# The sum over source heads moved to one contraction on TensorE, with amplitudes and values turned through DRAM

## What is computed

```python
# per token: q, k, v of 8 heads x 16; each head normed; q and k "entangled" in 3 depths -> complex
for c in range(4):                                   # circuits
    pattern = einsum('bsid,bsjd->bsij', conj(qa), ka)
    scores  = abs(mod) ** 2 * SCALING
    amps    = sqrt(softmax(scores, axis=-1) + 1e-12) # (tokens, 8 target heads i, 8 source heads j)
    weighted = einsum('bsij,bsjd->bsid', w, vq)      # sum over source heads j
    co = weighted * coh                              # coh turns by the phase of the sum of vq over heads
    amp = clip(abs(co), 1e-6, 1.0)                   # magnitude clipped, sign kept
    final = final + sup_w[c] * amp * exp(1j * phase)
return real(final) @ W_out.T + b_out
```

## Time and profile before

| what | value |
|---|---|
| median of 3 runs | 2482.29 us (2481.22 to 2492.06) |
| span of the profiled execution | 2447.5 us |
| busy in it: PE / PEld / DVE / ACT / POOL | 1901.8 / 1470.5 / 1872.7 / 1264.7 / 1562.1 us |
| residual x0 loads (one at the end of each iteration) | 96.67, 153.42, 216.18, then 28 more until 1909.46 us |

### The profile page before, as it was taken

The page is one execution under the profiler, slowest core; times in us unless marked ns, Lnnn a source line. Parts: engine busy times, 40 slices in busy tenths (PEclk is TensorE's granted clock), DMA queues, the critical chain, the costliest instruction groups (busy, mean ns, idle before and its releaser), DMA issues.

```text
span 2447.5 us, 42464 instructions
## 1 busy us (share of the span) xinstructions
PE 1901.8 (78%) x14044; PEld 1470.5 (60%) x14044; DVE 1872.7 (77%) x3303; ACT 1264.7 (52%) x2982; POOL 1562.1 (64%) x1233
## 2 busy tenths in 40 slices
PE   1478888888888888888888888888888877968490
PEld 0366666666666666666666666666666654746370
DVE  8989999998999999999999989999998742311010
ACT  2246666555556655555565555555555544423130
POOL 4656666666666666666666666666666215788787
PEclk9889999898999998999998989999989876989795
DMA  3000000000000000000000000000000001233233
GB/s 96 5 5 10 9 9 9 9 9 9 9 9 9 9 9 9 9 9 9 9 9 9 9 9 9 9 9 9 9 9 6 8 10 39 46 41 41 47 36 33
DMA packets 66108, 39.50 MB, mean 16 GB/s; under 512 B 10886, under 2 KB 61967, under 8 KB 66064
## 3 DMA queue, kind: packets, MB, share of 16 engines
q0 software_dynamic: 22528, 16.79, 5.2%
q1 hardware_dynamic: 43490, 22.12, 3.2%
q10 hardware_dynamic: 46, 0.00, 0.0%
HBM read 22.11 MB, written 16.78 MB: 16 GB/s over the span
## 4 chain that ended last, share of the span: by engine, by line
POOL 30%; issue 25%; DVE 21%; PE 17%; ACT 6%; DVEq 1%; POOLq 0%; ACTq 0%; DMA 0%
POOL out_x L1246 7%; POOL arena L481 5%; POOL arena L677 4%; POOL arena L649 4%; DVE arena L831 4%; PE pb L1056 3%; POOL arena L478 2%; POOL arena L1236 2%; PE pa L752 2%; PE pa L779 2%; POOL arena L682 1%; DVE arena L578 1%; DVE arena L583 1%; POOL arena L483 1%; PE pa L1335 1%
## 5 line engine op out<-in xcount | busy, mean ns | idle before, releaser
L771 PE MATMUL pa<-ident,arena 128*128 128x128 f32 x4096 | 531.9, 287 | 56.9 <-DVE arena L649 52.9
L771 PEld LDWEIGHTS pa<-ident,arena 128*128 128x128 f32 x4096 | 504.1, 201 | 74.2 <-DVE arena L649 36.1
L1056 PE MATMUL pb<-ident,arena 128*128 128x128 f32 x1536 | 289.9, 302 | 128.1 <-ACT arena L951 119.0
L1056 PEld LDWEIGHTS pb<-ident,arena 128*128 128x128 f32 x1536 | 187.0, 152 | 246.0 <-issue 158.8
L951 ACT ACTIVATE arena<-pb 128x384 f32<-128x384 f32 x512 | 253.0, 494 | 157.6 <-PE pb L1056 153.8
L677 POOL TENSOR_TENSOR arena<-state,c_cross 128x448 f32<-128x448 f32 x128 | 202.5, 1602 | 203.8 <-DVE state L538 199.1
L669 POOL TENSOR_TENSOR arena<-arena,neg_half 128x32 f32<-128x32 f32 x64 | 264.9, 4158 | 83.8 <-DVE arena L515 83.8
L649 POOL TENSOR_TENSOR arena<-arena 128x1024 f32<-128x1024 f32 x64 | 149.9, 2343 | 197.0 <-PE pa L771 197.0
L944 ACT ACTIVATE arena<-pd,arena 128x256 f32<-128x256 f32 x512 | 245.6, 480 | 0.0
L649 DVE TENSOR_TENSOR arena<-arena 128x1024 f32<-128x1024 f32 x192 | 236.1, 1256 | 2.5 <-PE pa L771 2.2
L1246 POOL DMA_INDIRECT out_x<-arena x128 | 201.9, 1577 | 39.0 <-issue 37.1
(11 more groups left out here) (244 smaller groups left out, 4314.0 us busy)
## 6 DMA issues: line engine op xcount, KB each, us to landing
x_land<-in_L_attn_query SPq DMA_DIRECT2D x32, 128.0 KB, 2.1
arena<-in_L_attn_query SPq DMA_DIRECT2D x32, 128.0 KB, 2.1
out_x<-x SPq DMA_DIRECT2D x32, 128.0 KB, 1.8
xn_scratch<-xn_d SPq DMA_DIRECT2D x32, 128.0 KB, 1.8
w<-in_L_ffn_W SPq DMA_DIRECT2D x1, 2048.0 KB
arena<-xn_scratch,arena POOLq DMA_INDIRECT x128, 2.5
out_x<-arena POOLq DMA_INDIRECT x128, 3.3
arena<-in_L_attn_W_qkv SPq DMA_DIRECT2D x1, 192.0 KB, 2.7
```

The costliest lines, as they stand in the source:

```text
L771: mm = pe.matmul(pa[:, t, c * P:c * P + P], wprod[:, k % NWP, j * 128:j * 128 + 128], ident[:, :], start=(j == 0), stop=(j == NH - 1))
L1056: mm = pe.transpose(pb[:, j * P:j * P + P], p_raw[:, s % 3, j * P:j * P + P], ident[:, :])
```

## The change

1. **Values.** In stage C, DVE now computes the sign of the sum of the values and flips them first (lines 588 to 590 after), then SP writes `v_enc` to DRAM (`send_values`) and reads it back with 16 DMAs (`spread_values`) into `v_diag`: 16 groups of 16 tokens-and-tiles, partitions (x, t, j), values in block-diagonal columns. The zeros off the diagonal are written once, in the setup.
2. **Amplitudes.** ACT writes them as (tile, source, circuit x target); SP sends them to DRAM (`send_amps`) and reads them back with one DMA of 128 x 16 pieces of 32 words (`spread_amps`) into `amps_t`.
3. **The sum.** PE contracts the 128 partitions (8 tokens x 2 tiles x 8 sources) at once: 16 groups x 4 strips of 32 columns, 64 matmuls with 64 moving columns. The 8 products of DVE and POOL, their buffers and the 64 matmuls against the identity are gone.
4. **Layout after the sum.** The output projection reads every eighth word of `clipped` as its stationary operand, against weights reordered in the setup (`wout_q`). It waits for both clipped halves.
5. **Smaller parts.** `prod` is reused for both tiles, the third product has its own buffer; `norm_scale` waits until its factors have been applied; a wait is added ahead of stage B's first statistics; all four order strings are new.

```diff
-        mag = first("mag", [P, T, NC * P])
-        clipped = first("clipped", [P, T, NC * P])
-        prod = first("prod", [P, T, 3, 1024])
-        wprod = first("wprod", [P, NWP, 1024])
+        amps = first("amps", [P, T, NH, CI])
+        mag = first("mag", [P, 2, 512])
+        clipped = first("clipped", [P, 2, 512])
+        prod = first("prod", [P, 2, 1024])
+        prod_third = first("prod_third", [P, T, 1024])
+        v_diag = first("v_diag", [P, NGRP, XG * HD])
+        amps_t = first("amps_t", [P, NGRP, CI])
 
         x1 = first("x1", [P, T, E])
         state = sb("state", [P, 2, T, 2, E])
...
+            v.memset(v_diag[:, :, :], 0.0).then_inc(S("v_diag_zero"), 1)
...
             link(v.tensor_scalar(sup_w[:, :], tmp[:, 48:52], tmp[:, 53:54], None, ALU.mult))
+            by_d = wout_s.rearrange("p (i q d) -> p q i d", q=NQ, d=DQ)
+            for d in range(DQ):
+                v.tensor_tensor(wout_q[:, d, :].rearrange("p (q c i) -> p q c i", q=NQ, c=NC),
+                                by_d[:, :, :, d].unsqueeze(2).broadcast_to([P, NQ, NC, NH]),
+                                sup_w[:, :].unsqueeze(1).unsqueeze(3).broadcast_to([P, NQ, NC, NH]),
+                                ALU.mult).then_inc(S("w_out_scaled"), 1)
...
             if not (isinstance(b, int) and b == 0):
-                v.wait_ge(S("a_wprod"), 6 * b)
-                v.wait_ge(S("a_wpool"), 2 * b)
+                v.wait_ge(S("v_out"), 16 * b)
...
+
+            v4 = v_enc[:, :, :].rearrange("p t (i d) -> p t i d", d=HD)
+            v.wait_ge(S("a_venc"), b + 1)
+            yield from L(v.tensor_reduce(v_sum[:, :, :], v_enc[:, :, :].rearrange("p t (i d) -> p t d i", d=HD), AX, ALU.add))
+            yield from L(v.tensor_scalar(v_sign[:, :, :], v_sum[:, :, :].bitcast(U32), SIGN, None, ALU.bitwise_and))
+            v.tensor_tensor(v4.bitcast(U32), v4.bitcast(U32), v_sign[:, :, :].unsqueeze(2).broadcast_to([P, T, NH, HD]),
+                            ALU.bitwise_xor).then_inc(S("a_signed"), 1)
+            yield
 
...
             yield
-
-            v.wait_ge(S("a_amps"), b + 1)
-            for t in range(T):
-                for c in range(NC):
-                    k = t * NC + c
-                    if k and k not in ON_POOL:
-                        yield
-
-                    if k not in ON_POOL:
-                        if k >= NWP:
-                            v.wait_ge(S("a_wsum"), 8 * b + k - NWP + 1)
-                        weighted(v, t, c).then_inc(S("a_wprod"), 1)
-                    if k == 6:
-                        yield
-                        yield from vector_clip(v, b, 0)
-            yield
-            yield from vector_clip(v, b, 1)
-            yield
+            for h in range(2):
+                yield from vector_clip(v, b, h)
+                yield
             v.wait_ge(S("a_y"), b + 1)
 
             v.wait_ge(S("x0_bias"), b + 1)
...
-            for n, k in enumerate(ON_POOL):
-                g.wait_ge(S("a_amps"), b + 1)
-                g.wait_ge(S("a_wsum"), 8 * b + k - NWP + 1)
-                weighted(g, k // NC, k % NC).then_inc(S("a_wpool"), 1)
                 yield
             g.wait_ge(S("x0_in"), 16 * b + 16)
             g.tensor_tensor(x0[:, :, :], x0[:, :, :], bout_v.unsqueeze(1).broadcast_to([P, T, E]), ALU.add)\
...
-            for t in range(T):
-                act.wait_ge(S("a_wsum"), 8 * b + 4 * t + 4)
-                act.activation(mag[:, t, :], pa[:, t, :], ACT.Abs).then_inc(S("a_mag"), 1)
+            if not (isinstance(b, int) and b == 0):
+                act.wait_ge(S("amps_out"), 16 * b)
+            act.activation(amps[:, :, :, :].rearrange("p t j c -> p t c j"), probs[:, :, :].rearrange("p (t c) j -> p t c j", t=T),
+                           ACT.Sqrt, bias=tiny[:, 0:1]).then_inc(S("a_amps"), 1)
+            yield
+            for h in range(2):
+                act.wait_ge(S("a_wsum"), 2 * b + h + 1)
+                act.activation(mag[:, h, :], pa[:, h, :], ACT.Abs).then_inc(S("a_mag"), 1)
                 yield
 
...
         def tensor_c(pe, b):
-            for t in range(T):
-                for c in range(NC):
-                    k = t * NC + c
-                    if k:
-                        yield
-                    elif not (isinstance(b, int) and b == B - 1):
-                        pe.wait_ge(S("a_qkvb"), b + 2)
-                    if k == 0 and not (isinstance(b, int) and b == 0):
-                        pe.wait_ge(S("x2_ready"), b)
-                    if k in ON_POOL:
-                        pe.wait_ge(S("a_wpool"), 2 * b + k // NC + 1)
-                    else:
-                        pe.wait_ge(S("a_wprod"), 6 * b + k - k // NC + 1)
-                    for j in range(NH):
-                        mm = pe.matmul(pa[:, t, c * P:c * P + P], wprod[:, k % NWP, j * 128:j * 128 + 128], ident[:, :],
-                                       start=(j == 0), stop=(j == NH - 1))
-                    mm.then_inc(S("a_wsum"), 1)
-            for t in range(T):
-                yield
-                pe.wait_ge(S("a_clip"), 2 * b + t + 1)
-                o = pa[:, t, 0:128]
-                for c in range(NC):
-                    mm = pe.matmul(o, clipped[:, t, c * P:c * P + P], w_out_t[:, c, :], start=(c == 0), stop=(c == NC - 1))
+            if not (isinstance(b, int) and b == B - 1):
+                pe.wait_ge(S("a_qkvb"), b + 2)
+            if not (isinstance(b, int) and b == 0):
+                pe.wait_ge(S("x2_ready"), b)
+            pe.wait_ge(S("v_spread"), 16 * XG * b + 16 * XG)
+            pe.wait_ge(S("amps_spread"), 16 * b + 16)
+            for h in range(2):
+                for g in range(NGRP // 2):
+                    n = NGRP // 2 * h + g
+                    of_row = v_diag[:, n, :].rearrange("p (x d) -> p x d", d=HD)
+                    for q in range(NQ):
+                        mm = pe.matmul(pa[32 * q:32 * q + 32, h, g * 64:g * 64 + 64].rearrange("p (x d) -> p x d", d=DQ),
+                                       amps_t[:, n, :], of_row[:, :, DQ * q:DQ * q + DQ], start=True, stop=True)
+                mm.then_inc(S("a_wsum"), 1)
+                yield
+            pe.wait_ge(S("a_clip"), 2 * b + 2)
+            of_tile = clipped[:, :, :].rearrange("p h (n k) -> p (h n) k", k=T * DQ)
+            for t in range(T):
+                for d in range(DQ):
+                    mm = pe.matmul(pa[:, t, 0:128], of_tile[:, :, t * DQ + d], w_out_t[:, d, :], start=(d == 0), stop=(d == DQ - 1))
             mm.then_inc(S("a_y"), 1)
             yield
 
...
+        def send_values(sp, b):
+            if isinstance(b, int) and b == 0:
+                sp.wait_ge(S("v_diag_zero"), 1)
+            else:
+                sp.wait_ge(S("a_wsum"), 2 * b)
+            sp.wait_ge(S("a_signed"), b + 1)
+            sp.dma_start(v_rows_d, v_enc[:, :, :].rearrange("p t n -> p (t n)")).then_inc(S("v_out"), 16)
+
+        def spread_values(sp, b):
+            sp.wait_ge(S("v_out"), 16 * b + 16)
+            of_row = v_rows_d.rearrange("(g x) (t j d) -> (x t) j g d", x=XG // T, t=T, d=HD)
+            for x in range(XG):
+                sp.dma_start(v_diag[NH * x:NH * x + NH, :, HD * x:HD * x + HD], of_row[x]).then_inc(S("v_spread"), 16)
+
+        def send_amps(sp, b):
+            sp.wait_ge(S("a_amps"), b + 1)
+            sp.dma_start(amps_d, amps[:, :, :, :].rearrange("p t j c -> p (t j c)")).then_inc(S("amps_out"), 16)
+
+        def spread_amps(sp, b):
+            sp.wait_ge(S("amps_out"), 16 * b + 16)
+            sp.dma_start(amps_t[:, :, :], amps_d.rearrange("(g x) (t j c) -> (x t j) g c", x=XG // T, t=T, c=CI)).then_inc(S("amps_spread"), 16)
 
         def sync_d(sp, b):
...
+                load_x0(sp, b)
             with sp.Fori(3, B - 1) as b:
                 load_x(sp, b + 1)
+                send_values(sp, b - 1)
+                spread_values(sp, b - 1)
+                send_amps(sp, b - 1)
+                spread_amps(sp, b - 1)
```

110 lines of the change are left out of this document (57 added, 53 removed).

## The result

The changed kernel takes **2500.11 us** (median of 20 runs, 2480.07 to 2507.88) against 2483.7 us for the kernel before: a ratio of **1.006 (95% interval 1.0043 to 1.0076)**, slightly slower, where 2253 us was forecast. The profiled execution spans 2500.6 us.

The account below looks back on a forecast made before the run. The loop was taken as bound by DVE's row of work plus a short serial tail; period 60.47 to 53.0 us saves 209, filling 21, last 3, setup -4, together 229: 2253 us, forecast range 2200 to 2295 us.

Parts of the forecast that it names:

- PE can't be the bound by its sum: PE's work in the loop: falls from 50 to 38 us an iteration, so its total cannot set the period.
- rival 2: PE's clock in second attention: 1.2 GHz for longer, chain about 4 us longer, period 57, 2374 us; chance 0.12.
- Rival 1: Projection's strided operand, line 768: doubling line 779's 3.35 us, period 56.4, 2360 us; chance 0.13.
- The walk's path: One iteration followed from probabilities at 28.0 us through POOL's crosses and stage D's norm to a 53.0 us period.
- My own check: Last drain iteration but one, without A and C: lasts 53.00 us at clock 0.78, so period not below 51.
- Products, and DVE's row: Products removed from DVE: 7.3 us an iteration, plus 0.6 of POOL's hold-up, leaving DVE 47.3 of 55.2 us.
- The contraction: PE's 64 new matmuls: taken as 4.5 us an iteration, between 4.2 and 6.7, running from 40 to 44.5.
- Transfers: Trips through DRAM: amplitudes spread between 35.3 and 39.0 us, hidden by 1 to 5 us; values hidden by twenty.
- rival 4: Small DMA pieces: hold SP 5.5 us each for values and amplitudes, land late, slower, up to 2599 us; chance 0.07.
- The second magnitude behind line 504: Sign of being right, iteration's end: ACT's second magnitude stands behind line 504, which waits for POOL.
- The sum: Whole kernel: 28 loop periods from 60.47 to 53.0 save 209 us, 229 with filling, last iteration and setup: 2253 us.
- the clock below 0.7 in the first 20 us: Sign of being wrong: granted clock under 0.7 in the first 20 us of iterations.

Follow-up runs that it names:

- e1: The kernel before with 8 of the 64 matmuls against the identity kept an iteration, all products and waits kept: 2539.33 us, ratio 1.024.
- e10: The changed kernel with 17 filling matmuls an iteration added in the second attention, six of them ahead of the third head's transposes: 2394.39 us, ratio 0.9639.
- e6: The changed kernel with the output projection's stationary operand read as 128 neighbouring words, result wrong: 2433.43 us, ratio 0.9805.
- e12: The changed kernel with the clip writing by output column, so the projection reads neighbouring words, result right: 2421.51 us, ratio 0.9756.
- e14: The changed kernel with filling matmuls in second attention (17) and stage D (13), and the clip written by output column: 2298.22 us, ratio 0.9268.
- e2: The kernel before with its eight weighted products cut to 16 elements each, all 64 matmuls and waits kept: 2401.13 us, ratio 0.9684.
- e5: The changed kernel with 1 of 16 pieces of the values and one sixteenth of the amplitudes read back: 2491.97 us, ratio 1.0039.
- e8: The changed kernel with the iteration's last instructions reordered on ACT, PE and DVE, second magnitude directly behind the first: 2526.1 us, ratio 1.0178.

## Why the prediction was wrong

- **"PE can't be the bound by its sum" and rival 2's size.** This is the step that failed. The mechanism was named (12 us less of dense matmuls, PE at 1.2 GHz for longer), with "half of the second attention", +4 us and a chance of 0.12. The forecast of 53.0 put the clock at nothing, and priced PE's path to the contraction as if its level stayed. Measured: 10.9 us more for PE's other work an iteration, stretches at 0.50 to 0.55 in second attention, stage D and the projection, some 33 us of 61, and PE at the contraction 49.0 us in, not 40. I had two rows that warned, 0.59 in the tail and 0.78 in the drain, and used them as local facts. e1 shows the cause without any of the change's other parts: the dense matmuls alone taken out make the kernel before 2.4% slower. e10 shows it from the other side: 17 useless matmuls make the changed kernel 4% faster. What exactly makes the clock fall behind one wait and not behind another stays open.
- **Rival 1, the stride,** with 0.13 was in part true as well. The doubling is real at the full clock, 4.08 against 2.05 us, but line 779's 3.35 us, which I doubled, was itself a row at a low clock (0.59). In the changed kernel all projections of the loop ran at 0.50 and took 4.15, and neighbouring words at that level take 3.76 (e6): a direct cost of 0.4. The period still fell by 2.5 and 3.0 us (e6, e12) when the operand was made contiguous, near the 3.4 of the rival, with a higher clock; the price was right by luck. I took nothing because DVE and ACT read strided views freely; that says nothing of a weight load. The Trainium skill ("SBUF — State Buffer", section "Door 1: The DMA port swizzle") has reads pay at each new 16-byte line; the operand with 32 bytes of stride did pay, and the trace agrees there. Two rivals that I had taken as unlikely and separate were both there.
- **The walk's path.** The probabilities were ready at 1037.54 - 1004.01 = 33.5 us, not at 28.0; even in e14, at clock 0.94, they are ready at 30.2. The path that ended the iteration was not POOL's crosses but scores, transposes and copies of the second attention, then stage D. PE reached the contraction 49.0 us in, not at 40. In e14 it is 44.2, so some 4.8 of these 9.0 us went with the higher clock, and 4.2 are the walk's own: "about 3 us, my estimate" for the last heads stood on no row (17 added matmuls lie in that stretch of e14 too). My own check, 53.00 us for the drain without A and C, was the sign that this chain alone is as long as my whole period.
- **Products, and DVE's row:** right. 47.35 us busy predicted as 47.3. The gain could not be had because it was no longer DVE that waited least.
- **The contraction:** priced 4.5, measured 3.06 at a clock of 0.64 and 2.12 in e14. The 5.8 us of e2 show that the old form, at a clock of 0.94, would have held DVE up as well.
- **Transfers:** hidden, as forecast; rival 4 didn't come. The trace has them landed 6 us early, and e5 moved the loop by 0.02 us in ten iterations.
- **The second magnitude behind line 504:** seen as foretold (1057.80, then 1058.58), yet moving it, with the rest of the iteration's end (e8), brought a loss.
- **The sum:** 53.0 predicted, 61.44 measured, 8.4 apart. Clock and stride together are 6.8 of it (61.44 to 54.64 in e14, with the filling's own cost in it); the other 1.6 were not taken apart. The repaired kernel, at 2298 us, lies inside the range given for the change, but it is another kernel, with 30 matmuls more and another clip, and doesn't bear the forecast out.

By the signs I had written down: the loads of x0 were to be 53 us apart (61.44), PE busy 38 (48.7), and "the clock below 0.7 in the first 20 us" was to be the sign of failure: it was 1.00 for 13 us and 0.51 for the next ten. "Line 768 above 4 us at granted clock 1" was never seen in the changed kernel's loop (4.15 at 0.50). The signs for the transfers, for DVE (47.35) and for the second magnitude came as written.
